# Router weights carried with the gathered token rows, and a combination that adds while it gathers

## The reference, cut to what matters

```python
logits = x @ gate_w.T                                  # 2048 tokens, 64 experts
topv, topi = jax.lax.top_k(logits, TOP_K)              # TOP_K = 8
rw = jax.nn.softmax(topv, axis=-1)
W = zeros((N, E)).at[arange(N)[:, None], topi].set(rw)
gate, up = einsum('nh,eih->nei', x, gu_w)              # 64 + 64 columns an expert
inter_w = silu(gate) * up * W[:, :, None]
out = einsum('nei,ehi->nh', inter_w, dp_w)
out = out + sigmoid(x @ sh_gate1_w.T) * sh_out         # shared expert
x = x + gb * out
...
mod = (_silu(L1_c) @ L1_wmod).reshape(2, 6, 1, -1)     # layer 1: six rows of 256 per batch
h = _layernorm(x) * (1 + ca) + sa                      # layer 1 begins
```

## Time and profile before

| | us |
|---|---|
| median of 3 runs | 1233.77 (1231.28 to 1235.89) |
| the profiled execution, its own time | 1234.32 |
| its span, first to last instruction | 1232.6 |
| routing, first one-hot product to its last (L1108) | 172.48 to 212.83 |
| units (L1120 first, last store issued) | 221.70 to 489.2 |
| combination, first gather to last DVE instruction | 492.28 to 667.76 |

### The profile page before, as it was taken

One profiled execution on the slowest core, in us unless ns is written; L12 is line 12 of the kernel. 1 busy time (PEld: TensorE's weight loads), 2 busy tenths in 40 slices (PEclk: granted clock), 3 DMA queues, 4 the chain that ended last, 5 costly groups with the idle time before them and its releaser, 6 DMA issues. The chain is left out here.

```text
span 1232.6 us, 17414 instructions
## 1 busy us (share of the span) xinstructions
PE 971.5 (79%) x5364; PEld 629.4 (51%) x5364; DVE 782.5 (63%) x2247; ACT 519.0 (42%) x1131; POOL 525.2 (43%) x548
## 2 busy tenths in 40 slices
PE   7899889899999998000002989999988889999887
PEld 6666745677777776000001543333332367688565
DVE  6468897255454433366545588888887569877465
ACT  3221366344444443000001546777767462534553
POOL 3110068776666662777774542111111243453000
PEclk9989975899999999555555999999999999999899
DMA  4060160666666665533331741233311300110001
GB/s 156 1 271 18 51 140 16 174 200 192 191 194 192 190 191 162 164 101 97 99 96 52 234 135 49 70 83 74 74 19 25 118 26 27 51 53 1 1 18 51
DMA packets 74521, 125.00 MB, mean 101 GB/s; under 512 B 12282, under 2 KB 52288, under 8 KB 73024
## 3 DMA queue, kind: packets, MB, share of 16 engines
q1 hardware_dynamic: 58944, 81.80, 21.7%
q0 software_dynamic: 15360, 41.96, 12.3%
q10 hardware_dynamic: 128, 0.13, 0.0%
HBM read 83.80 MB, written 35.66 MB: 97 GB/s over the span
## 5 line engine op out<-in xcount | busy, mean ns | idle before, releaser
L1546 POOL DMA_INDIRECT h_t<-modulated_rows,ga_rows x192 | 181.7, 946 | 81.5 <-PE ps L1120 41.1
L2033 DVE CUSTOM_DVE_ANT_0 masked<-ps,causal 128x128 f32<-128x128 f32 (+7 forms) x256 | 181.1, 755 | 40.7 <-PE ps L1832 39.8
L145 PE MATMUL ps<-consts,xn 128*128 128x128 f32 x128 | 19.6, 303 | 185.0 <-PEq L78 104.2
L1558 POOL DMA_INDIRECT big<-expert_rows,slot x128 | 126.0, 985 | 60.4 <-issue 40.5
L2013 ACT ACTIVATE xn<-ps 128x512 f32<-128x512 f32 (+3 forms) x256 | 111.7, 511 | 44.5 <-PE ps L1854 43.6
L1465 DVE SCALAR_TENSOR_TENSOR xn<-big,weights,xn 128x256 f32<-128x256 f32 x128 | 62.4, 488 | 84.1 <-DMA big<-expert_rows,slot 80.1
L145 PEld LDWEIGHTS ps<-consts,xn 128*128 128x128 f32 x128 | 16.5, 158 | 190.0 <-issue 109.9
L1275 ACT COPY h_t<-ps 128x512 f32<-128x512 f32 x96 | 56.3, 586 | 126.4 <-PE ps L1120 126.3
L1162 PE MATMUL ps<-room,rows_b 64*128 x384 | 108.0, 402 | 0.0
L1451 DVE COPY h_t<-ps 128x512 f32<-128x512 f32 x96 | 66.4, 692 | 65.3 <-PE ps L1162 64.5
L1140 PE MATMUL ps<-big,h_t 128*128 x768 | 102.3, 276 | 0.0
(11 more groups left out here) (322 smaller groups left out, 2221.1 us busy)
## 6 DMA issues: line engine op xcount, KB each, us to landing
expert_rows<-h_t SPq DMA_DIRECT2D x96, 256.0 KB, 2.3
qk<-qk_parts SPq DMA_DIRECT2D x72, 128.0 KB, 2.7
big<-in_gu SPq DMA_DIRECT2D x8, 1024.0 KB, 11.4
qk_parts<-parts SPq DMA_DIRECT2D x16, 384.0 KB, 2.6
raw<-in_mlp SPq DMA_DIRECT2D x16, 384.0 KB, 3.1
room<-in_down SPq DMA_DIRECT2D x4, 1024.0 KB, 10.8
h_t<-modulated_rows,ga_rows POOLq DMA_INDIRECT x192
h_t<-qk_parts SPq DMA_DIRECT2D x24, 128.0 KB, 2.8
```

The lines of the kernel that those rows point to most:

```text
L1546: nc.gpsimd.indirect_dma_start(xg[:, u % 4, i, :], None, row_dram, bass.IndirectOffsetOnAxis(ap=idxg[:, 2 * u + i:2 * u + i + 1].bitcast(U ...
L1558: nc.gpsimd.indirect_dma_start(yg[:, t % 2, k, :], None, y_dram, bass.IndirectOffsetOnAxis(ap=slots[:, n:n + 1].bitcast(U32), axis=0))\
L2033: nc.vector.tensor_tensor_reduce(masked[:, at % 2, 0:k], ps[:, bank:bank + (k + GW - 1) // GW, :] .rearrange("p a n -> p (a n)")[:, 0:k], ...
```

## The change

- The DRAM row of a token grows from 256 to 320 numbers (1024 to 1280 bytes): its 64 normalised router weights, zero for experts not chosen, stand behind it. POOL masks and normalises them in two instructions, and SP stores them with one more DMA, of 2048 pieces of 256 bytes. ACT's wait before the one-hots now counts this store too.
- In a unit DVE picks the weight of each slot by a copy of one column at an offset taken from a register (the expert's number), and the copy out of PSUM becomes two multiplications by that column. The extraction of weights in the units goes away.
- The combination's gathers add into `xn` themselves, each waiting for the one before on the same tile; tiles are taken in groups of four, choice by choice. DVE keeps the gate and the residual.
- Layer 1's modulation weights are loaded in twelve chunks of 128 KB during the units and used there by DVE; layer 1's q, k and v weights are loaded at unit 4.
- `KP` is 3: ACT makes five of the eight row one-hots, POOL three.

The diff, cut (a line "..." where something is left out; twelve leading spaces are taken off):

```diff
-        row_dram = nc.dram_tensor("modulated_rows", (T, D), F32, kind="Internal").ap()
+        row_dram = nc.dram_tensor("modulated_rows", (T, D + E0), F32, kind="Internal").ap()
...
+parts4 = sb(st, "slot_parts", [P, 4 * NT * TOPK])
+row_f, tile_f, nrow_f, part_f = [parts4[:, n * NT * TOPK:(n + 1) * NT * TOPK] for n in range(4)]
+part_i = part_f.bitcast(I32)
+w_chunk = parts4[:, :].rearrange("p (s d) -> p s d", s=2)
+c_row = m16[:, :, :].rearrange("p t e -> p (t e)").bitcast(F32)
 spread = sb(st, "spread", [P, 2 * UNITS0])
-w8 = sb(st, "weights8", [P, NT, TOPK])
-w_scr = sb(st, "weight_scratch", [P, 4, E0])
+wcol = sb(st, "slot_weight", [P, 8, 2])
+expert = sb(st, "expert_int", [1, 2 * UNITS0], I32)
...
+xg = flat_h[:, 0:8 * RW].rearrange("p (s i d) -> p s i d", s=4, i=2)
+hs = [flat_h[:, 14 * D:16 * D], swap[:, 6 * D:8 * D]]
+ys = flat_h[:, 8 * RW:8 * RW + 4 * D].rearrange("p (s i d) -> p s i d", s=2, i=2)
...
-KP = 4
+CHUNK0 = 8
+KP = 3
...
+        sp.wait_ge(s_wd, 1)
+        sp.dma_start(row_dram[:, D:].rearrange("(t p) e -> p t e", p=P), ex[:, :, :]).then_inc(s_xst, 16)
         sp.wait_ge(s_l, NT)
         sp.dma_start(room[0:H, RING:], a["down0"][:, RING:]).then_inc(s_wdn, 16)
         for u in range(UNITS0):
+            if u == 4:
+                sp.dma_start(c_row, a["c1"].to_broadcast([P, BATCH * D])).then_inc(s_c1, 16)
+                for n, w in enumerate(("wq1", "wk1", "wv1")):
+                    sp.dma_start(wqkv1[:, n], a[w].rearrange("(k p) n -> p k n", p=P)).then_inc(s_w1, 16)
+            if u >= CHUNK0 and (u - CHUNK0) % 4 == 0 and (u - CHUNK0) // 4 < 12:
+                c = (u - CHUNK0) // 4
+                if c >= 2:
+                    sp.wait_ge(s_modf, 2 * c - 2)
+                sp.dma_start(w_chunk[:, c % 2, :], a["wmod1"][:, c * D:(c + 1) * D]).then_inc(s_wm[c % 2], 16)
             sp.wait_ge(s_ye, u + 1)
             sp.dma_start(y_dram[u * 2 * P:(u + 1) * 2 * P, :].rearrange("(i p) d -> p i d", p=P),
                          ys[:, u % 2, :, :]).then_inc(s_yst[u % 2], 16)
-        sp.dma_start(w_row, a["wmod1"]).then_inc(s_wmod1, 16)
-        sp.dma_start(c_row, a["c1"].to_broadcast([P, BATCH * D])).then_inc(s_wmod1, 16)
-        for n, w in enumerate(("wq1", "wk1", "wv1")):
...
+            nc.scalar.activation(pos[:, 4 * g:4 * g + 4, :], pos[:, 4 * g:4 * g + 4, :], ACT.Exp)
...
-        act.wait_ge(s_xst, 16 * NG)
+        act.wait_ge(s_xst, 16 * (NG + 1))
...
+            if i == CHUNK0:
+                act.wait_ge(s_c1, 16)
+                nc.scalar.activation(c_row, c_row, ACT.Silu).then_inc(s_mod1, 1)
...
+            nc.vector.tensor_tensor(pos[:, ts, :], top[:, ts, :], bc(top[:, ts, 0], 2, TOPK),
...
+        link(nc.vector.tensor_reduce(zsum[:, :], pos[:, :, :], AX.X, ALU.add))
+        nc.vector.reciprocal(zsum[:, :], zsum[:, :]).then_inc(s_z, 1)
...
-        def weight(n):
-            t, k = divmod(n, TOPK)
-            if n >= 4:
-                dve.wait_ge(s_wt, n - 3)
-            nc.vector.scalar_tensor_tensor(w_scr[:, n % 4, :], key[:, t, :], pos[:, t, k:k + 1],
-                                           ex[:, t, :], ALU.is_equal, ALU.mult,
-                                           accum_out=w8[:, t, k:k + 1]).then_inc(s_wt, 1)
+        def conditioned(c):
+            dve.wait_ge(s_mod1, 1)
+            dve.wait_ge(s_wm[c % 2], 16 * (c // 2 + 1))
+            for b in range(BATCH):
+                i = c * BATCH + b
+                if i >= 1:
+                    dve.wait_ge(s_modf, i)
+                nc.vector.tensor_tensor_reduce(bv[:, :], w_chunk[:, c % 2, :], c_row[:, b * D:(b + 1) * D],
+                                               1.0, 0.0, ALU.mult, ALU.add,
+                                               accum_out=modc[:, 1, c, b:b + 1]).then_inc(s_modf, 1)
+        def guarded(part):
+            step = mod_link(dve)
+            dve.wait_ge(s_modf, 12 * part + 12)
+            m = modc[:, 1, 6 * part:6 * part + 6, :]
+            guard(m[:, 4:6, :], (gtmp[:, 1, part, 0], gtmp[:, 1, part, 1]), step)
+            nc.vector.tensor_scalar(m[:, 2:4, :], m[:, 2:4, :], 1.0, None, ALU.add).then_inc(s_modr, 1)
+        column = {}
         for i in range(UNITS0 + 3):
+            u = i
+            if u < UNITS0:
+                if u % 2 == 0:
+                    _, values4 = nc.values_load_multi_w_load_instructions(
+                        expert[0:1, 2 * u:2 * u + 4], engines=(mybir.EngineType.DVE,), min_val=0,
+                        max_val=E0 - 1,
+                        skip_runtime_bounds_check_because="the expert number is clamped when it is written")
+                    for n, v in enumerate(values4):
+                        column[2 * u + n] = v
+                dve.wait_ge(s_xg[u % 4], 32 * (u // 4 + 1))
+                for n in range(2):
+                    last = nc.vector.tensor_copy(wcol[:, u % 8, n:n + 1],
+                                                 xg[:, u % 4, n, bass.ds(column[2 * u + n] + D, 1)])
+                last.then_inc(s_wc, 1)
...
+                dve.wait_ge(s_wc, u + 1)
                 if u >= 2:
                     dve.wait_ge(s_yst[u % 2], 16 * (u // 2))
-                nc.vector.tensor_copy(ys[:, u % 2, :, :],
-                                      ps[:, 6 + u % 2, :].rearrange("p (i d) -> p i d", i=2)).then_inc(s_ye, 1)
-            if 8 <= i < 8 + NT * TOPK // 2:
-                for n in range(2 * (i - 8), 2 * (i - 8) + 2):
-                    weight(n)
-        dve.wait_ge(s_wt, NT * TOPK)
-        link(nc.vector.tensor_reduce(zsum[:, :], w8[:, :, :], AX.X, ALU.add))
-        link(nc.vector.reciprocal(zsum[:, :], zsum[:, :]))
-        link(nc.vector.tensor_tensor(w8[:, :, :], w8[:, :, :], bc(zsum[:, :], 2, TOPK), ALU.mult))
+                for n in range(2):
+                    last = nc.vector.tensor_scalar(ys[:, u % 2, n, :], ps[:, 6 + u % 2, n * D:(n + 1) * D],
+                                                   wcol[:, u % 8, n:n + 1], None, ALU.mult)
+                last.then_inc(s_ye, 1)
+            c = i - CHUNK0 - 6
+            if c >= 0 and c % 4 == 0 and c // 4 < 12:
+                conditioned(c // 4)
+            if i in (UNITS0 - 20, UNITS0 - 19):
+                guarded(i - (UNITS0 - 20))
...
         def combine(t):
-            dve.wait_ge(s_yg[t % 2], 16 * TOPK * (t // 2 + 1))
-            for k in range(TOPK):
-                link(nc.vector.scalar_tensor_tensor(xn[:, t, :], yg[:, t % 2, k, :], w8[:, t, k:k + 1],
-                                                    xn[:, t, :], ALU.mult, ALU.add))
+            dve.wait_ge(s_yg[t], 16 * TOPK)
...
-            if 1 <= t < 7:
-                conditioned(t - 1)
-            if t in (7, 8):
-                guarded(t - 7)
             if t in (3, 7):
                 dve.wait_ge(s_ac, t + 1)
                 ln_stats(t // 4, link)
-            if t in (5, 9):
-                ln_rows(dve, (t - 5) // 4, s_early, 2)
+                ln_rows(dve, t // 4, s_early, 2)
...
+        pool.wait_ge(s_exd, NG)
+        pool.wait_ge(s_m, NG)
+        made(nc.gpsimd.tensor_tensor(ex[:, :, :], ex[:, :, :], m16[:, :, :], ALU.mult))
+        pool.wait_ge(s_z, 1)
+        nc.gpsimd.tensor_tensor(ex[:, :, :], ex[:, :, :], bc(zsum[:, :], 2, E0), ALU.mult).then_inc(s_wd, 1)
+        pool.wait_ge(s_wd, 1)
...
+                pool.wait_ge(s_wc, u - 3)
...
-        pool.wait_ge(s_gu, UNITS0)
+        pool.wait_ge(s_she, NT)
         for n in range(2):
             pool.wait_ge(s_yst[n], 16 * (UNITS0 // 2))
-        for t in range(NT):
-            if t >= 2:
-                pool.wait_ge(s_ac, t - 1)
+        for g in range(NG):
             for k in range(TOPK):
-                n = t * TOPK + k
-                nc.gpsimd.indirect_dma_start(
-                    yg[:, t % 2, k, :], None, y_dram,
-                    bass.IndirectOffsetOnAxis(ap=slots[:, n:n + 1].bitcast(U32), axis=0))\
-                    .then_inc(s_yg[t % 2], 16)
-            if t in (5, 9):
-                ln_pool(pool, 2, ((t - 5) // 4,))
+                for t in range(4 * g, 4 * g + 4):
+                    n = t * TOPK + k
+                    if k:
+                        pool.wait_ge(s_yg[t], 16 * k)
+                    nc.gpsimd.indirect_dma_start(
+                        xn[:, t, :], None, y_dram,
+                        bass.IndirectOffsetOnAxis(ap=slots[:, n:n + 1].bitcast(U32), axis=0),
+                        compute_op=ALU.add).then_inc(s_yg[t], 16)
+                if g in (1, 2) and k == 2:
+                    ln_pool(pool, 2, (g - 1,))
...
```

55 lines of the change are left out of this document (14 added, 41 removed).

## The result

The changed kernel takes 1320.89 us (median of 4 runs, 1317.75 to 1327.72) against 1233.79 us before (4 runs on the same chip): ratio 1.071, 95% interval 1.068 to 1.074. The forecast was 1235, with 1227 to 1280 as its range. The profiled execution has a span of 1319.1 us against 1232.6: 86.5 us to be found.

| | before | after | difference |
|---|---|---|---|
| first one-hot product | 172.48 | 185.93 | +13.4 |
| from it to the end of the last one | 40.35 | 37.57 | -2.8 |
| from there to DVE's last copy of a unit, ended | 276.3 | 281.7 | +5.4 |
| from there to the first gather | 3.1 | 2.9 | -0.2 |
| first gather to last gather (start) | 167.7 | 237.9 | +70.2 |

A forecast was written before the change was run, and what follows sets the result against it. PE was taken to bound the units, POOL's gather issuing the combination, and a chain started by POOL's one-hots routing. Combination -10.5, routing +10.2 and units +1.2 gave +0.9 us: forecast 1235.0 us, range 1227 to 1280.

The forecast's parts named there:

- the price of the adding gather: Combination, POOL: an adding gather was taken to cost the plain gather's 0.948 us, so 0 extra.
- Its upper bound, 0.474: Combination, POOL: a second read entry per row makes each gather 1.5 times as long, 0.474 us more, 60 us over 127.
- the whole case: Combination: POOL pays for the second read, +30 us at half the upper bound, 1295 us at the bound; chance 27%.
- The combination at the plain price: Combination, POOL: without DVE's interference and waits, first to last gather takes 160.9 us against 167.7, 6.8 us less.
- The end: Combination, after the last gather: DVE's eight additions go, -4.2 us; the last landing comes later, +0.5 us.
- The wait for the fifth store: Routing: ACT waits for the router weights' store, queued behind a load, landing at 179.5; first one-hot product +10.7 us.
- DVE gets 0.7 us of small new instructions ahead of the slots; the wait hides them: Routing, DVE: 0.7 us of new instructions, hidden by ACT's longer wait for the router weights' store.
- The pace: Routing, one-hot tiles: 2.56 us each against 2.59, so -0.5 us over 15 tiles.
- Units: Unit stage: +1 us for loads and ACT's wait, +0.2 for the last copy; DVE's new steps hidden under PE's 2.76 us.
- ACT's wait: Units, at unit 8: ACT waits for the first of four loads issued at unit 4, between 0 and 4 us, taken as +1.
- The Trainium skill's rule of two reads: Combination transfers: two read descriptors per chunk, about half the rate; engine share from 33.1% to some 66%, still hidden.

The follow-up runs named there:

- the half gathers: Changed kernel gathering only the first 64 of each tile's 128 rows in the combination: 1374.62 us with adding gathers, 1320.15 us with plain ones.
- the first four kernels: Run together: changed with plain gathers 1313.55 us, before with adding gathers 1338.37, changed with 64-row gathers adding 1374.62 or plain 1320.15; before beside them 1280.03.

## Why the prediction was wrong

The step that failed is the price of the adding gather: "Nothing in the rows splits 946 ns into a fixed part and a part per row; I take the nearest row, the plain gather, hence 0." Measured it is +0.60 us, times 127 starts 76 us, and it alone puts the time outside the range. Its upper bound, 0.474, failed as well: it came from a picture (one more entry per row) and not from a row, and the half gathers show a cost that is mostly not of that kind. The text had said that 0.05 us would decide and gave 27% to the whole case; an operation that stands in no row, multiplied by 127 on the engine that never waits, called for the upper half as the middle of the forecast.

By its other steps:

- **The combination at the plain price.** Forecast 160.9 us from the first gather to the last; without the addition it was measured at 161.8. That DVE's interference goes is right. It is worth 6 us, and the addition costs twelve times that.
- **The end.** Forecast -4.2 + 0.5; measured -3.1, since the last landing takes 1.0 longer, not 0.5.
- **The block's end** was missed: +3.1. POOL's drain, the last thing that the next block waits for, ends 2.5 us after the last gather's record before, where DVE's additions cover it, and 6.3 after it now. The kernel before, and then the changed one:

```profile
L914 POOLq DRAIN  x1: 15267/15267/15267, 648.1 to 648.1; - x1
```

```profile
L913 POOLq DRAIN  x1: 11409/11409/11409, 742.4 to 742.4; - x1
```

  They end at 663.4 and 753.8. The kernel before with adding gathers has the same 6.3; the changed one without the addition has 8.2. So the addition isn't what lengthens it. With half the rows it is longer still (9.4 and 14.9), which suggests that the drain holds work that the gathers' records leave out; no run shows it. What sets its length is open.
- **The wait for the fifth store.** The mechanism was right, the sum right by luck: routing as a whole was forecast at +10.2 and measured at +10.6, the landing at 179.5 and 181.9. The store costs 2.2 us behind the load's landing (173.86 + 5.8 = 179.7), 1.8 in two other traces, not 5.5, and the load lands 1.0 us sooner after its issue; but it goes out 6.6 us later. By the Trainium skill, "DMA: Bandwidth & Descriptors", section "Why small descriptors are slow (HBM only)", the store was estimated at 1.8 us; the traces (1.8 to 2.2) agree with it far better than with the 5.5 of the row that was preferred, a load of other small pieces.
- **"DVE gets 0.7 us of small new instructions ahead of the slots; the wait hides them"**. The size was right: with POOL's products away the load goes out 0.6 us later than before. That the wait hides them was wrong, because they don't lie under the wait but move its start. And two terms were missing: POOL's products beside DVE's old instructions (1.5 + 1.3 us), and PE's clock, which fell while PE waited for DVE (2.7). The first could have been read ahead, from the row at 165.25 in the trace of before.
- **The pace.** Forecast -0.5, measured -2.8: -0.8 by the work (2.54 us a tile at the lower clock, 2.59 before), -2.0 by the clock, which was above its lower level for part of the stage. That is luck: in another execution of the same instructions it wasn't.
- **Units.** Forecast +1.2, measured +5.4. ACT's wait was foreseen "between 0 and 4"; it is 4.45, and the clock from 260 to 280 us is 0.93. The steady period stayed at 2.76 us, with DVE at 1.36 us a unit (134.96 us of 273): the many small steps are hidden, as forecast.
- **The Trainium skill's rule of two reads**, from "Collectives: The Full Stack", section "The bandwidth ceiling: the fold count and why AG ≠ RS ≠ AR": the engines' time per gather doubled, from 0.45 to 0.503 x 242 / 128 = 0.95 us, as by the rule. But the packets also became 1 KB instead of 4 KB, so the runs don't tell whether the second read or the smaller packets doubled it. It was as hidden as forecast. The rule bears on the transfer; the loss lay with the engine that issues it.

What stays open: the fixed 0.44 us of POOL (0.36 by the stages) and what it does in them, POOL's drain, the 3.4 us of the units behind ACT's wait, and the longer units of the first four kernels. There the changed kernel with plain gathers takes 328.9 us from first to last `turn` and the kernel before with adding ones 293.5, 35 apart; in the traces of the result it is 264.1 and 259.0.

## What to carry to other kernels

Moving work off an engine that waits wins its exposed part, here 4 us, and what it disturbed on the engine that bounds the stage, here 6. A semaphore per transfer won most of the first without moving anything. Before an operation is put 128 times on the engine that never waits, have one instruction of it measured: here a flag on an instruction added 63% to its time. Where a store or load is put ahead of a wait, follow its issue back: what delays the issuing chain counts as much as the transfer. And where work is given to POOL, look in the trace for DVE instructions beside its present work that are longer than their like elsewhere: this trace had one.
